# Convolution of a selective-scan layer computed in two phases of tokens, with a new slot table

## The reference, cut to what matters

```python
xc, z = split(layernorm(x) @ in_proj_w.T)           # 512 inner channels each
h = conv1d(pad(xc, 3 in front), conv_w) + conv_b     # full 512 x 512 x 4 taps
u = h.T                                              # what everything below reads
dt = clip(sigmoid(u @ dt_w.T + dt_b)); Bm = u @ B_w.T; Cm = u @ C_w.T
state = exp(clip(dt*A)) * state + dt*B*u + 1e-6      # 16 states for each channel
y = (sum over states of state*C + D*u) * silu(z)
x = x + y @ out_w.T
```

## Time and profile before

| | us |
|---|---|
| median of three runs | 1482.96 (1481.94 to 1483.48) |
| the profiled execution's own time | 1485.81 |
| its span, first to last instruction | 1484.0 |
| of it: attention, first experts | 0 to 409.6 |
| last taps, statistics, preparation of sequence 0 | 409.6 to 481.88 |
| the slots (first scan to last) | 481.88 to 1277.87 |
| end of the layer, routing, second experts | 1277.87 to 1484.0 |

### The profile page before, as it was taken

How to read it: one execution, slowest core, us unless ns; L and a number is a source line. 1 busy time by engine, 2 the same in 40 slices (tenths; PEclk the granted TensorE clock), 3 DMA queues, 4 the chain that set the end, 5 groups by cost and what they waited for, 6 DMA issues and landing times.

```text
span 1484.0 us, 22146 instructions
## 1 busy us (share of the span) xinstructions
PE 1371.3 (92%) x6998; PEld 959.5 (65%) x6998; DVE 1011.4 (68%) x1529; ACT 937.4 (63%) x1737; POOL 860.9 (58%) x436
## 2 busy tenths in 40 slices
PE   5999998999998998998999999989999887989997
PEld 3566695999844555565565655655656576559996
DVE  6666615333241799898899898998998997853332
ACT  1222221344323999899899998998999998314442
POOL 1111002455300799798898898898988978325552
PEclk9999968999999999999999999999999979999999
DMA  9200033666430499797997998989979989376662
GB/s 300 82 28 28 29 87 119 195 210 208 139 109 16 95 220 204 167 218 178 194 224 178 205 221 185 210 192 196 222 168 200 230 192 214 91 237 201 213 210 82
DMA packets 108229, 248.39 MB, mean 167 GB/s; under 512 B 19097, under 2 KB 49950, under 8 KB 94048
## 3 DMA queue, kind: packets, MB, share of 16 engines
q0 software_dynamic: 23104, 131.96, 41.0%
q1 hardware_dynamic: 82944, 113.68, 25.6%
q10 hardware_dynamic: 2080, 1.47, 0.3%
HBM read 116.72 MB, written 18.94 MB: 91 GB/s over the span
## 4 chain that ended last, share of the span: by engine, by line
PE 67%; ACT 14%; DVE 10%; issue 5%; DMA 2%; SPq 1%; another core or an unknown queue 1%; ACTq 0%; DVEq 0%; POOLq 0%; POOL 0%
PE ps L1299 11%; PE ps L1512 9%; PE ps L1566 9%; PE ps L1503 9%; PE ps L1597 7%; ACT arena L744 6%; ACT arena L754 6%; PE ps L1324 4%; DVE arena L1196 3%; PE ps L1639 3%; PE ps L1361 2%; PE ps L1583 2%; PE ps L1628 2%; PE ps L1448 2%; PE ps L1418 2%
## 5 line engine op out<-in xcount | busy, mean ns | idle before, releaser
L499 POOL TENSOR_TENSOR arena<-arena 128x2048 f32<-128x2048 f32 x91 | 424.3, 4671 | 124.0 <-DVE arena L1196 116.3
L1299 PEld LDWEIGHTS ps<-cst,arena 128*128 128x128 f32 x2428 | 300.2, 146 | 288.7 <-issue 182.2
L1196 DVE TENSOR_TENSOR_SCAN arena<-arena,ps 128x512 f32<-128x512 f32 x364 | 432.0, 1210 | 67.8 <-PE ps L1299 64.1
L1299 PE MATMUL ps<-cst,arena 128*128 128x128 f32 x2428 | 370.7, 282 | 63.8 <-ACT arena L754 29.3
L744 ACT ACTIVATE arena<-arena,a_neg 128x512 f32<-128x512 f32 x512 | 366.2, 715 | 44.7 <-DVE arena L1196 30.7
L754 ACT ACTIVATE arena<-arena,m_bt 128x512 f32<-128x512 f32 x512 | 363.0, 710 | 3.5 <-DVE arena L1133 1.8
L1566 PE MATMUL ps<-arena,tapw 128*128 128x512 f32 x512 | 261.2, 613 | 0.7 <-ACT arena L692 0.7
L1196 DVE TENSOR_TENSOR_SCAN x<-arena,ps 128x512 f32<-128x512 f32 x148 | 175.8, 1209 | 22.0 <-PE ps L1299 20.6
L499 POOL TENSOR_TENSOR x<-x,arena 128x2048 f32<-128x2048 f32 x36 | 169.7, 4714 | 16.7 <-DVE x L1196 13.7
L1077 DVE TENSOR_TENSOR arena<-ps,arena 128x256 f32<-128x256 f32 x78 | 33.1, 425 | 207.5 <-PE ps L1512 125.3
L455 POOL DMA_INDIRECT arena<-rows,arena x78 | 75.7, 971 | 165.2 <-DVE arena L1057 142.1
(11 more groups left out here) (162 smaller groups left out, 1565.2 us busy)
## 6 DMA issues: line engine op xcount, KB each, us to landing
arena<-arena POOLq DMA_DIRECT2D x52, 1024.0 KB, 8.3
arena<-in_W SPq DMA_DIRECT2D x94, 512.0 KB, 8.1
arena<-c_rows SPq DMA_DIRECT2D x128, 256.0 KB, 3.7
arena<-x POOLq DMA_DIRECT2D x28, 1024.0 KB, 8.2
x<-arena POOLq DMA_DIRECT2D x24, 1024.0 KB, 8.3
rows<-x SPq DMA_DIRECT2D x16, 512.0 KB, 4.0
x<-residual SPq DMA_DIRECT2D x12, 512.0 KB, 5.9
x<-in_x SPq DMA_DIRECT2D x8, 512.0 KB, 11.1
```

The costliest lines, as they stand in the source:

```text
L499: g.tensor_tensor(h, h, m_c[i % RC].unsqueeze(1).to_broadcast([P, KI, SEQ]), ALU.mult)\
L1196: v.tensor_tensor_scan(out=h[:, k, :], data0=m_a[g % RA], data1=ps[SCAN_BANK[g % 3]][:, :], initial=0.0, op0=ALU.mult, op1=ALU.add).then_i ...
L1299: return t.transpose(bank, src[:, k * P:(k + 1) * P], ident)
```

## The change

**Three products of two taps for four.** The tokens of a sequence are taken in even and odd phase. For each output block there are now three parts of four products each (2 blocks d x 2 steps j), each of 256 tokens instead of 512: part 0 multiplies every second token of `m_xt` by sums of neighbouring taps, and gives what both phases share; parts 1 and 2 multiply differences of neighbouring tokens by single taps, one part for each phase. So an output block takes 12 products of 256 tokens in place of 8 of 512.

**What it needs besides.** POOL makes the tap sums once (four additions of 128x1024, `sum_taps`) and the differences for every sequence (`m_differ`, two subtractions of 128x512 that read every second token, after the last C product of a sequence). ACT evicts part 0 with the bias to the odd places of `m_u` (`m_both`, 256 elements in place of 512). DVE has a new operation for each output block, `m_join`: it adds this shared part to the two phases in PSUM and interleaves them (128x512, PSUM read with a step of 256 elements).

**Rows of x.** The ring of four is replaced by one place for the rows of the norm (`rows_in`) and one for those of the update (`kept`), loaded apart (`ld_rows`, `ld_late`); the place freed holds tap sums and differences. Rows of sequences 4 and 5 are loaded again for the last routing, into the taps' buffer, late in the scans of sequence 6. Semaphores of the expert stages are shared between both stages.

**New slot table.** Nearly all tables are new. PE: CONV_AT has 4 products in slots 0 and 1, none in 2 to 4, and the other 44 in slots 5 to 23, up to five in one slot.

```diff
-CONV_AT = ((0, 1, 2, 2, 3, 4, 5, 6), (7, 8, 8, 10, 11, 12, 13, 14), (14, 15, 16, 17, 18, 20, 21, 21), (22, 23, 24, 26, 28, 29, 30, 30))
-UT_AT = (12, 19, 25, 34)
-OUT_AT = ((23, 25, 25, 26, 28, 29, 32, 33), (38, 39, 41, 43, 43, 47, 49, 49))
-BC_AT = (19, 23, 27, 34)
-DT_AT = ((33, 34, 36, 36), (37, 38, 39, 40), (43, 44, 45, 47), (48, 49, 50, 51))
-UC_AT = (10, 18, 25, 32)
-ADD_AT = ((7, 8, 10, 15), (12, 14, 14, 17))
-FINAL_AT = (13, 15, 17, 21)
-SKIP_AT = (3, 5, 8, 16)
+CONV_AT = ((0, 0, 0, 1, 6, 6, 7, 7, 8, 8, 9, 9), (5, 6, 6, 6, 10, 10, 11, 11, 11, 11, 13, 13), (14, 14, 15, 15, 15, 16, 16, 16, 17, 17, 18, 18), (19, 20, 20, 20, 20, 21, 21, 21, 22, 22, 23, 23))
+UT_AT = (12, 17, 25, 28)
+OUT_AT = ((22, 25, 25, 25, 27, 27, 28, 31), (36, 38, 40, 42, 43, 45, 47, 49))
+BC_AT = (27, 28, 29, 30)
+DT_AT = ((31, 32, 32, 33), (34, 35, 36, 37), (42, 42, 42, 43), (45, 46, 47, 48))
+N_LOAD = 8
+JOIN_AT = (9, 15, 20, 24)
+UC_AT = (3, 7, 16, 20)
+DIFFER_AFTER = 15
+ADD_AT = ((5, 6, 13, 16), (11, 12, 15, 17))
+FINAL_AT = (11, 15, 18, 20)
+SKIP_AT = (2, 4, 12, 17)
...
+            def sum_taps(out, j):
+                g.tensor_tensor(out[:, j], tapw[:, TAPS - 1 - 2 * j], tapw[:, TAPS - 2 - 2 * j], ALU.add)\
+                    .then_inc(S("m_zero"), 1)
...
+            def m_differ(n):
+
+                g.wait_ge(S("m_xtc"), KD * (n + 1))
+                for s in range(2):
+                    g.tensor_tensor((m_xd if n else xd_first)[:, s], m_xt[n % 2][:, :, PAD + 1 - 2 * s:PAD + SEQ - 2 * s:2],
+                                    m_xt[n % 2][:, :, PAD:PAD + SEQ - 1:2], ALU.subtract).then_inc(S("m_xd"), 1)
...
-            def m_uevac(n, o):
-                a.wait_ge(S("m_umm"), KI * n + o + 1)
+            def m_both(n, o):
+
+                a.wait_ge(S("m_umm"), conv_done(n, o, BOTH_END))
                 if n >= 2:
                     a.wait_ge(S("m_y0"), KI * (n - 2) + o + 1)
-                a.activation(m_u[n % 2][:, o, :], ps[CONV_BANK[o]][:, :], ACT.Identity, bias=mvec[:, 0, o:o + 1])\
-                    .then_inc(S("m_u"), 1)
+                a.activation(m_u[n % 2][:, o, 1::2], both_bank(n)[:, o % 2 * HALF:(o % 2 + 1) * HALF], ACT.Identity,
+                             bias=mvec[:, 0, o:o + 1]).then_inc(S("m_both"), 1)
...
+            def m_join(n, o):
+
+                v.wait_ge(S("m_both"), KI * n + o + 1)
+                v.wait_ge(S("m_umm"), conv_done(n, o))
+                u = m_u[n % 2][:, o, :].rearrange("p (t s) -> p t s", s=2)
+                v.tensor_tensor(u, ps[CONV_BANK[o]][:, :].rearrange("p (s t) -> p t s", s=2),
+                                u[:, :, 1].unsqueeze(2).to_broadcast([P, HALF, 2]), ALU.add).then_inc(S("m_u"), 1)
...
-                d, k = i // TAPS, i % TAPS
-                mm = t.matmul(ps[CONV_BANK[o]][:, :], tapw[:, k, d, o * P:(o + 1) * P], m_xt[n % 2][:, d, k:k + SEQ],
-                              start=(i == 0), stop=(i == TAPS * KD - 1))
-                if i == TAPS * KD - 1:
+                if part == 0:
+                    out, lo = both_bank(n), o % 2 * HALF
+                    w = (tap_sum if n else sum_first)[:, j, d, o * P:(o + 1) * P]
+                    mm = t.matmul(out[:, lo:lo + HALF], w, m_xt[n % 2][:, d, PAD - 2 * j:PAD - 2 * j + SEQ - 1:2],
+                                  start=first, stop=last)
+                else:
+                    out, lo = ps[CONV_BANK[o]], (2 - part) * HALF
+                    w = tapw[:, TAPS - part - 2 * j, d, o * P:(o + 1) * P]
+                    mm = t.matmul(out[:, lo + j:lo + HALF], w, (m_xd if n else xd_first)[:, part - 1, d, 0:HALF - j], start=first, stop=last)
+                if i in (BOTH_END, PARTS - 1):
                     mm.then_inc(S("m_umm"), 1)
```

More of the change, by code:

```diff
@@ L34 @@
 PAD = TAPS - 1
+HALF = SEQ // 2
+TURN_OF = ((0, 0), (0, 1), (1, 1), (1, 0))
+PARTS, BOTH_END = 3 * len(TURN_OF), len(TURN_OF) - 1
 LN_EPS, NORM_EPS = 1e-5, 1e-6
@@ L278, in build @@
                   for w in (m_dt[0].rearrange("p k t -> p (k t)"), u_raw[0]) for i in range(2)]
+        staged += [tapw[:, k].rearrange("p d n -> p (d n)").rearrange("p (c d) -> p c d", c=CPB) for k in range(2)]
         x_turned = ([f_xt[i % 2] for i in range(BATCH)], [halves[i // IN_LAST][i % 2] for i in range(BATCH)])
@@ L293, in kept, with conv_done, tiles_done, rows_in @@
         def kept(b):
-            return CPB * (b % RING)
+            return CPB if b == BATCH - 1 else 0
+        conv_marks = [(o, i) for q in range(SLOTS) for o in range(KI) for i in range(PARTS)
+                      if CONV_AT[o][i] == q and i in (BOTH_END, PARTS - 1)]
+        def conv_done(n, o, i=PARTS - 1):
+            return len(conv_marks) * n + (conv_marks.index((o, i)) + 1 if n else 2 * o + 1 + (i == PARTS - 1))
+        def tiles_done(r, par):
+            return r * (TURNS + 1 - par)
+        def rows_in(n):
+            return CPB if n else 0
         def place(b):
@@ L517, in _ @@
                     add_on(i)
+                if i % NS == DIFFER_AFTER and i // NS < BATCH - 2:
+                    m_differ(i // NS + 2)
             for lo, at in ((0, RING * CPB), (RING * CPB, 0)):
@@ L684, in m_norm @@
                 i = CPB * n + c
-                a.activation(m_xn[:, c % XN, :], x[:, kept(n) + c, :], ACT.Identity, bias=nw[2][:, i:i + 1],
+                a.activation(m_xn[:, c % XN, :], x[:, rows_in(n) + c, :], ACT.Identity, bias=nw[2][:, i:i + 1],
                              scale=rstd[:, i:i + 1]).then_inc(S("m_xn"), 1)
@@ L1174, in m_pre @@
             def m_pre(n, q):
+                if n and q in JOIN_AT:
+                    m_join(n, JOIN_AT.index(q))
                 if q in CLIP_AT:
@@ L1265, in _ @@
             v.wait_ge(S("ld_mid1"), 16 * (BATCH - 1))
-            m_stats(CPB, NCH)
+            for c in range(CPB, NCH // 2):
+                row_stats(c)
+            m_join(0, 0)
+            for c in range(NCH // 2, NCH - 1):
+                row_stats(c)
+            link(row_stats(NCH - 1))
+            m_join(0, 1)
+            layer_norm_scales(CPB, NCH)
+            shifts(CPB, NCH)
+            m_join(0, 2)
+            m_join(0, 3)
             for q in range(SLOTS):
@@ L1409, in x_turn @@
                     for k in range(KD):
-                        rows = staged[b][:, c, :] if r and b < RING else x[:, (kept(b) if r else CPB * b) + c, :]
+                        rows = staged[b][:, c, :] if r and b < BATCH - 2 else x[:, (kept(b) if r else CPB * b) + c, :]
                         last = turned(ps[FEED_PAIR[r][i][k]][:, c * P:(c + 1) * P], rows, k, c)
@@ L1657, in m_prep @@
                 for o in range(KI):
-                    for i in range(TAPS * KD):
+                    for i in range(PARTS):
                         if q == CONV_AT[o][i]:
@@ L1718, in _ @@
             for o in range(KI):
-                for i in range(TAPS * KD):
+                for i in range(PARTS):
                     m_conv(0, o, i)
-                    if o and i == TAPS:
+                    if o and i == PARTS // 2:
                         m_uturn(0, o - 1)
```

135 lines of the change are left out of this document (84 added, 51 removed).

## The result

The changed kernel takes 1494.61 us (median of 7 runs, 1488.24 to 1501.26), the kernel before 1482.96 us in the same comparison (7 runs, 1477.17 to 1484.85): ratio 1.0089, 95% interval 1.0058 to 1.0119. It is slower by 11.7 us, with the interval clear of 1; 1464 was forecast, 19 us faster.

The account below looks back on a forecast made before the run. No engine alone bounds a period; the fullest changes by piece of eight slots, PE in the middle ones. Gains 9.0 + 3.5 + 6.7 = 19.2 us, taken from 1482.96, give 1463.8, about 1464; range 1455 to 1472, chance 0.60.

Parts of the forecast that it names:

- Moved loads: Reload of sequences 4 and 5 near slot 56 of sequence 6, wanted at slot 2 next: 0 to 4 us late, taken as 0.
- (e) DMA: About one more 0.5 MB load a period, costed at nothing; POOL's 4.7 us product was to hide a late C row.
- the 9.0 us of periods 1 to 6: Gain in the six full periods, 1.5 us each, from 6.7 us less PE work a period.
- The first piece: First eight slots of a period: largest load in the new table ACT's, 11.7 us, so the piece takes that.
- A period, 97.8: Sum of the largest engine loads of a period's eight pieces of eight slots under the new tables: 97.8 us.
- Period 0, 3.5 less: First period, without closing work: 94.8 us before by the sums (94.2 measured), 91.3 after, 3.5 less.
- Preparation, 6.7 less: Sequence 0's preparation, PE alone: 64 passes of 0.43 us become 96 of 0.217, 6.7 us less.
- Prices: Costs per instruction in a stream: 256-token pass 0.217 us, 512-token pass 0.43, join 0.60 with upper bound 0.95.
- the rival of strided reads: Part 0's passes, reading every second token, cost 0.434 us: period 100.0, total 1489, slower; chance 0.06.
- The weight loads: Rival: 96 loads for 64 each add 0.19 us before their pass, PE 102.7 a period, about 1520; chance 0.01.
- The clock's rival: PE at low clock at seven boundaries: 2.7 us each gives 1476, twice that 1495; slower by the clock 0.05.
- slot 7's transposes at 11.0: Rival of POOL's late differences: PE waits at slot 6, about 1.3 us late, 1473; shares 0.14 for small gain.

Follow-up runs that it names:

- the loads apart: Changed kernel with the reloads of sequences 4 and 5 issued separately, sequence 7's x rows later, and PE's wait narrowed: 1485.52 us, ratio 1.0023.
- the last kernel: Changed kernel with moved loads, half loads, all additions later and last-sequence transfers in halves, those of sequences 2 and 3 after C rows 5 to 8: 1474.82 us, 0.9970.
- the later additions: Changed kernel with first two even additions in slots 7 and 8 for 5 and 6: 1493.87 us; all additions later, with moved loads: 1486.37.
- the halves: Kernel with moved loads, half loads and later additions, plus every last-sequence transfer of rows cut to 256 KB, at most one behind each C row: 1474.66 us, 0.9983.
- the filler: Changed kernel with 13 unread products a period on PE in slots 2 to 4 and 61 to 63, to keep its clock up: 1491.57 us.
- half loads: Moved-loads kernel with the 512 KB x load split into 256 KB after C rows 7 and 8: 1484.35 us; with all additions later 1478.52.
- moved loads and later even additions: Changed kernel with reloads apart and first two even additions in slots 7 and 8: 1488.42 us, ratio 1.0041; with filler 1487.46, ratio 1.0040.
- the kernels of the last halves: Kernel with moved loads, half loads, later additions and last-sequence transfers in halves: 1474.66 us; the same with filler in slots 61 to 63: 1490.95.

## Why the prediction was wrong

- **Moved loads, "0 to 4 us late, taken as 0"**: the step that failed most, 14.9 us in the last sequence. PE's wait was 9.94 us. The landing times went up to 17.1 us, but were read as those of one load issued at slot 56. The loads went out some 4 us later than that (1167.9 for 1163.5), behind a store that SP waits for; three went out together, of which the second took 18.6 us; and PE's wait asked for both reloads. Nothing in the prediction stood for the C row behind them, which held POOL for 13.83 us. That this is the cause is shown for 7.4 us of it (113.5 to 106.1 with the loads apart). The rest was gone in the last kernel (99.7), but for the later additions and the halves the parts are not settled, as said above.
- **(e) DMA, "costed at nothing", with "POOL's product of 4.7 us" as cover**: failed, and with it the 9.0 us of periods 1 to 6. The bandwidth part was right (a quarter of the bytes changes nothing), the cover was not: a C row behind 512 KB lands after 10.0 us, which is more than the 7.6 us from its issue (1030.39) to the moment when POOL could take it (1040.51 - 2.48). It costs the six periods 6 us (599.3 to 593.1) and more where it falls badly (606.2 in the changed kernel).
- **The first piece, 11.7 us by ACT's load**: mis-sized; 14.4 was measured, 12.3 with all repaired. The piece was sized by loads where waits set it: POOL late from the period before (12.6 and 12.9 without that, 13.1 to 14.3 with it, in one execution), PE behind at the boundary (slot 0 takes 2.7 to 3.4 us, three products at half clock) and the even chain's transfer at slot 5. With the filler slot 0 fell by 1.6 and the first piece by 0.7; with the later additions slot 5 fell by 2.5 and the first two pieces by 0.9. So each leaves most of its wait to the next.
- **A period, 97.8**: 98.9 with all repaired. The sum of the other seven pieces (86.1) was 86.6 in the changed kernel as after repair; single pieces were off by up to 1.1 both ways (12.8 and 12.6 for 11.7 and 11.7, 11.1 and 12.0 for 12.1 and 13.0). Against the 602.0 of before, 593.6 is 8.4 less, where 9.0 was predicted. In part that is luck: both periods are some 1 us longer than their sums (100.3 for 99.3 and 98.9 for 97.8), and the old order took 599.2 in another execution.
- **Period 0, 3.5 less**: failed, 94.5 for 94.2, and 95.2 after repair. Its last piece took 14.1 us for 11.9, with the late C row in it: PE waits there for POOL's norms (the timeline at 559.13), and slot 57 falls from 3.1 to 1.7 us with half loads. But then the seventh piece takes 12.6 for 11.5, and two middle pieces are longer in both (10.9 to 11.5, 11.6 to 12.1); no run looked for the cause.
- **Preparation, 6.7 less**: 7.1, right. The moment of the first scan varies between executions (466.2 to 475.8 in kernels that share this stretch, 481.9 and 477.1 in the old one), but mostly by what stands ahead of the convolution. From the first convolution pass to the first scan it is 62.3 and 61.2 us in the old order, 55.8 in the changed kernel and 53.3 to 55.4 in its edits.
- **Prices**: right. The groups of after, by form, from 880 to 1175:

```profile
L1670 PE MATMUL ps<-x,tapw 128*128 128x256 f32 x96 | 29.7, 397 | 10.2 <-ACT arena L783 5.3 <-POOL x L547 4.8
...
L1665 PE MATMUL ps<-arena,x 128*128 128x256 f32 x86 | 26.1, 431 | 0.0
...
L1192 DVE TENSOR_TENSOR arena<-ps,arena 128x512 f32<-128x512 f32 x12 | 8.1, 673 | 0.0
L547 POOL TENSOR_TENSOR x<-arena 128x512 f32<-128x512 f32 x6 | 7.1, 1358 | 0.0
```

The join is 0.673 us a record, as forecast. Back to back, part 0's passes follow at 0.229 us and the others at 0.216, so the rival of strided reads is out; its passes average 431 ns for 397, with a median of 390, since many of them stand at the boundaries, where the clock is low. By the Trainium skill (Advanced Engine Details and Errata, SBUF Cachelines) every second float32 should read at full speed; the trace agrees within 6%. The weight loads stay hidden (0.19 us each beside passes at 0.216). The Trainium skill (TensorE: Matmul & The Clock Gate, The mechanism) says that a load overlaps matmuls in flight only when it goes to another row group; the trace disagrees, as in the prediction. A difference took 1.36 for 1.17.

- **The clock's rival** named 1495 us and the time is 1494.6, but by another way: slot 0 does lose 1.6 us to it at a boundary, yet lifting the clock saved nothing (1487.46 with it for 1488.42 without, with moved loads and later even additions; 1490.95 for 1474.66 in the kernels of the last halves). That agreement is chance.
- **Small slips in the working**: the eight pieces of the period before add up to 99.4, not 99.3, and slot 7's transposes at 11.0 are 1.5 us later than 7/8 of 10.9, not 1.3. Neither changes a step.

In the last kernel the profiled execution is 13.7 us under that of before (1472.12 for 1485.81). Both lie aside of their medians, 2.7 below and 2.9 above, which leaves 8.1. The medians of the comparison on one chip give 5.5 (1480.36 to 1474.82), the ratio of 0.9970 gives 4.4. So the forecast of 19.2 would still have been far too large. Period 0 explains 4.5 us of that (1.0 more for 3.5 less); what else the executions without a trace lose is not shown.

## What to carry over

A transfer has a place in a queue besides its bytes: before moving or adding one, list what is issued behind it, when each of these is wanted, and how long the largest in front takes to land; here cutting loads in halves, with the same bytes, was worth 6 us in the periods. Look also at what a wait asks for: PE stood for two loads where it needed one. Before trusting a table of loads for a stretch between two phases, ask for the latest of the long chains that end in it. Less work for an engine was no gain until the transfers around it were put in order, and 0.3% then. One traced execution of each kernel does not settle differences of 1 us a period; several kernels on each side, or late and timely periods inside one execution, do.

## What was not expected of the hardware

- A C row of 256 KB lands after a median of 3.8 us, and after 7.6 to 11.4 us when a transfer of 512 KB was issued 6 us ahead of it on the same queue, while the accumulating transfers of 1 MB share the engines (they land in 9.0 to 9.5 us after, 8.2 to 8.3 before). Behind three such transfers it took 17.6 us.
- The share of the transfer engines is 0.90 in the periods of both kernels, and dropping 0.75 MB of 20 in a period changed the landing times (9.6 to 8.5 us) but not the periods (593.1 and 594.8).
- At the boundaries of the changed kernel PE stood at the 1.2 GHz level for 3.4 or 6.8 us, from within or just after a wait of 2.7 to 3.5 us for ACT's inputs. Before the last sequence it fell to it at 1172.6, in a wait of 2.5 us for ACT's inputs, and stood there for 17 us, in which the wait of 9.9 us for rows lies.
